# One class of candidates per row for strips 0 to 13, unsure rows settled in the tail, other gather lots

## Chip, core and metric

The kernel runs on one core of a Trainium2 chip. The metric is device time in microseconds (us), the median of several runs. Engines are named as in the profile: PE (matmul; PEld its weight loads), DVE (vector), ACT (scalar), POOL (GpSimd) and SP, whose queue loads the matrix.

## What is computed

The reference takes x (8192 x 64) and a sparse weighted adjacency matrix adj (8192 x 8192, float32, 268 MB) and applies two layers, each on a layer-normalised and rectified h:

```python
h = jnp.maximum(_layernorm(x, axis=-1), 0.0)
x = x + tanh([h, t] @ W1 + b1) @ W2 + b2 + adj @ (h @ B.T) - rowsum(adj) * (h @ B.T)
h = jnp.maximum(_layernorm(x, axis=-1), 0.0)
feats = h @ W                                   # 8 heads of 8
scores = leaky_relu(a_self[i] + a_neigh[j]) - 1e10 * (1 - adj[i, j])
x = x + relu(softmax_j(scores) @ feats + bias)
```

The mask is 1e10 times one minus the weight. Where the largest weight of a row leads the second by enough, the softmax is one at that neighbour and zero elsewhere, so the second layer is a gather: row i takes relu(feats + bias) of the column with its largest weight.

## The kernel before

**Strips.** The matrix, transposed and tiled on the host, comes in 16 strips (S) of 512 rows (W), each in 8 chunks of 2 MB, into a ring of four buffers. SP issues a load (L313 to L318) when PE (pe_chunk), ACT (half_done) and DVE (pair_done) are through with the buffer. A strip has four rows per partition (TB = 4).

**Per chunk.** PE multiplies it by h (`products`, L1032) and sums its rows (L1040, or L1050 on pairs that DVE added, L731). ACT casts it to float16 (`halve`, L544), and DVE folds the casts into a running maximum (`fold_chunk`, L738 and L742). DVE's order in a strip is written by hand (`strip`): pairs 0 and 1, the first fold, the candidates of the strip two back, the second fold, the classes of the strip before, and so on.

**Finding the largest weight.** Folding leaves, for each row, the maximum of each of 128 classes of 64 neighbouring columns. `search_classes` finds the top classes in float16 (L765, L769) and writes the row numbers of the first two (cls_row, L773). POOL fetches those two classes, 64 floats each, from adj in float32 (`fetch_rows`, L447): eight indirect DMAs of 128 rows of 256 B a strip. `search_candidates` finds the maximum of the 128 candidates (L786, L790) and the column, into best (L793 to L798).

**The gather.** relu(feats + bias) of each strip is stored to agg_dram (`store_agg`, L442). From strip 11 on POOL's order is written out: WINDOWS gives lots (known, t0, t1). In each, POOL adds b2 (L436), fetches half of the candidates of strip `known`, waits for the gathers of the previous lot, stores strip known - 1, fetches the rest, and gathers rows t0 to t1 per partition (L461) from the table, in which strips below `known` are stored. Rows whose best lies in a later strip read zeros and are late; up to SLOTS = 8 of them per partition are gathered after the last store (L490) and added to the output with a scatter (L499).

**The tail.** After the loop: `search_candidates(14)`, `search_classes(15)`, `residual(15)` (L806 to L819, waits for ACT's copy L602 of PE's results L1073 to L1080), `scale_h1` (L823, waits for ACT's deviation L615, L617), then the list of late rows (L887 to L908), agg_last (L912), its store by SP (L337), POOL's late gathers, scatters and last gathers, DVE's last addition (L918), and a test that the short cut held (L931 to L957). If it did not, a general path runs, which is slow.

## Time and profile before

| | us |
|---|---|
| median of 3 runs | 792.81 (790.75 to 794.08) |
| the profiled execution | 791.36 |
| its span, first to last instruction | 789.6 |
| busy: PE, DVE, ACT, POOL | 684.5, 652.1, 594.3, 388.5 |

Mean granted TensorE clock 0.948. A page has parts by number: 2 is the span in 40 slices, 3 the DMA queues, 5 groups of instructions with the idle time of the engine before them and what ended it. A timeline lists instructions in order of time; "x4" merges four.

### The profile page before, as it was taken

Reading aid. Unit: us, or ns where it says so; the run is one execution under the profiler, and the core shown is the slowest. Engines: PE = TensorE matmul, PEld = TensorE weight load, DVE = VectorE, ACT = ScalarE, POOL = GpSimd, SP = SyncE. Lnnn points to the kernel's source line nnn. Section 1 sums busy time; section 2 is a strip of 40 time slices with the busy share of each in tenths; the row PEclk is TensorE's granted clock in tenths of the full one; section 3 lists DMA queues with packets and bytes.
Section 4 is the critical chain, followed back from the end, with each engine's and each line's share of the span. In section 5 each row is a group of like instructions: output and inputs, shape, how many; then the busy total and the mean of one; then the engine's idle time right before and its main releaser. Section 6 shows DMA issues by size and latency. Waiting matters only on the chain.

```text
span 789.6 us, 13173 instructions
## 1 busy us (share of the span) xinstructions
PE 684.5 (87%) x4470; PEld 244.7 (31%) x4470; DVE 652.1 (83%) x944; ACT 594.3 (75%) x507; POOL 388.5 (49%) x281
## 2 busy tenths in 40 slices
PE   4899999999999999999999999999999999992100
PEld 1233333333333233333333333323233333332000
DVE  4586899999999989989899999999988989893420
ACT  3798888898879798888888887979797878880200
POOL 7000544434170807051443526070888888887574
PEclk9999999999999999999999999999999999995555
DMA  8999899999999999999999999999999999951161
GB/s 329 415 417 430 340 429 395 420 397 422 399 403 432 377 429 377 432 375 432 375 423 399 424 389 415 431 376 430 366 423 388 427 392 411 416 200 28 35 122 20
DMA packets 34544, 287.02 MB, mean 363 GB/s; under 512 B 7456, under 2 KB 13968, under 8 KB 18016
## 3 DMA queue, kind: packets, MB, share of 16 engines
q1 hardware_dynamic: 23168, 275.00, 84.4%
q0 software_dynamic: 9056, 9.73, 4.9%
q10 hardware_dynamic: 2304, 2.10, 0.8%
q8 instruction: 7, 0.11, 0.1%
q14 instruction: 9, 0.07, 0.0%
HBM read 279.46 MB, written 7.34 MB: 363 GB/s over the span
## 4 chain that ended last, share of the span: by engine, by line
PE 34%; DMA 27%; DVE 16%; issue 15%; ACT 3%; POOL 3%; DVEq 1%; SPq 0%; POOLq 0%; ACTq 0%
DMA ring<-in_adj_t 26%; PE acc L1032 22%; DVE work L742 6%; PE row_sums L1040 4%; PE row_sums L1050 4%; DVE work L731 4%; ACT work L544 2%; POOL out L499 2%; DVE work L738 1%; POOL work L490 1%; DVE work L748 1%; DVE idx_cls L769 1%; PE ps_xb L1080 1%; PE ps_acc L1073 1%; DMA work<-agg_dram,late_from 1%
## 5 line engine op out<-in xcount | busy, mean ns | idle before, releaser
L544 ACT CAST work<-ring 128x4096 f16<-128x4096 f32 x128 | 458.6, 3603 | 64.4 <-DMA ring<-in_adj_t 26.3
L1032 PE MATMUL acc<-ring,x_pb 128*64 128x512 f32 x2048 | 455.9, 596 | 14.8 <-DMA ring<-in_adj_t 14.8
L447 POOL DMA_INDIRECT cand<-in_adj,cls_row x128 | 226.7, 1771 | 86.9 <-DVE cls_row L773 49.0
L742 DVE TENSOR_TENSOR work<-work 128x4096 f16<-128x4096 f16 x96 | 221.6, 2309 | 22.5 <-ACT work L544 19.5
L1032 PEld LDWEIGHTS acc<-ring,x_pb 128*64 128x64 f32 x2048 | 140.4, 137 | 318.2 <-issue 280.1
L731 DVE TENSOR_TENSOR work<-ring 128x2048 f32<-128x2048 f32 x90 | 208.8, 2334 | 8.0 <-DMA ring<-in_adj_t 3.6
L442 POOL DMA_DIRECT2D agg_dram<-agg x15 | 9.0, 601 | 228.4 <-ACT agg L577 185.2
L461 POOL DMA_INDIRECT gathered<-agg_dram,best x64 | 85.5, 1336 | 20.9 <-issue 20.9
L1050 PE MATMUL row_sums<-work,ones_cols 128*32 128x512 f32 x720 | 89.5, 598 | 0.2 <-DVE work L731 0.2
L1040 PE MATMUL row_sums<-ring,ones_cols 128*32 128x512 f32 x608 | 72.9, 616 | 14.0 <-DMA ring<-in_adj_t 14.0
L436 POOL TENSOR_TENSOR x_tq<-x_tq,b_row 128x256 f32 (+1 forms) x16 | 30.4, 1902 | 42.5 <-DMA x_tq<-in_x 42.3
L738 DVE TENSOR_TENSOR work<-work 128x4096 f16<-128x4096 f16 x16 | 36.6, 2286 | 2.3 <-ACT work L544 2.3
L1040 PEld LDWEIGHTS row_sums<-ring,ones_cols 128*32 128x32 f32 x608 | 19.4, 112 | 57.2 <-issue 53.9
L1050 PEld LDWEIGHTS row_sums<-work,ones_cols 128*32 128x32 f32 x720 | 18.7, 109 | 54.3 <-issue 54.2
L615 ACT ACTIVATE tmp<-cen 128x64 f32<-128x64 f32 x64 | 15.6, 244 | 20.9 <-DVE cen L819 14.5
L602 ACT COPY acc_tq<-ps_acc 128x260 f32<-128x260 f32 x16 | 5.9, 369 | 24.8 <-remote 24.4
L1095 PE MATMUL ps_hid<-ident,h 128*128 128x128 f32 x2 | 0.7, 434 | 25.4 <-DVE rstd L823 25.4
L806 DVE TENSOR_TENSOR tmp<-ps_xb,acc_tq 128x256 f32<-128x256 f32 x16 | 6.7, 417 | 19.2 <-issue 19.2
L748 DVE TENSOR_TENSOR work<-work 128x2048 f16<-128x2048 f16 x16 | 19.6, 1225 | 2.3
L562 ACT ACT_TABLE_LOAD x16 | 20.5, 1283 | 0.3
L617 ACT ACT_TABLE_LOAD x16 | 20.5, 1283 | 0.3
L918 DVE TENSOR_TENSOR gathered<-gathered,x_tq 128x256 f32<-128x256 f32 (+1 forms) x3 | 4.7, 1573 | 18.5 <-DMA gathered<-agg_dram,best 18.5
(140 smaller groups left out, 503.7 us busy)
## 6 DMA issues: line engine op xcount, KB each, us to landing
ring<-in_adj_t SPq DMA_DIRECT2D x128, 2048.0 KB
agg_dram<-agg POOLq DMA_DIRECT2D x20, 128.0 KB, 20.1
x_tq<-in_x SPq DMA_DIRECT2D x1, 2048.0 KB, 16.3
cand<-in_adj,cls_row POOLq DMA_INDIRECT x128
raw_dram<-feat_stage ACTq DMA_DIRECT2D x16, 128.0 KB, 9.6
out<-gathered SPq DMA_DIRECT2D x1, 1792.0 KB
x_pb<-in_x SPq DMA_DIRECT2D x1, 1536.0 KB, 14.5
gathered<-agg_dram,best POOLq DMA_INDIRECT x64
```

Source lines behind the costliest of these rows:

```text
L436: pool.tensor_tensor(x1, x1, b2_row[:, :].unsqueeze(1).to_broadcast([P, TB, D]), ALU.add).then_inc(x_b2_done, 1)
L447: pool.indirect_dma_start(out=cand[:, k, g * NB:(g + 1) * NB], out_offset=None, in_=classes, in_offset=bass.IndirectOffsetOnAxis(ap=cls_ro ...
L461: pool.indirect_dma_start(out=gathered[:, t, :], out_offset=None, in_=agg_dram, in_offset=bass.IndirectOffsetOnAxis(ap=best[:, t:t + 1], a ...
L544: act.copy(half_chunk[c % 2], slot(c)).then_inc(half_done, 1)
L562: act.activation(hidden[:, :], ps_hid[:, :], ACT.Tanh, bias=hid_bias[:, 3:4])\
L731: dve.tensor_tensor(pairs[i % PBUF], slot(c)[:, 0:HALF], slot(c)[:, HALF:2 * HALF], ALU.add)\
L738: dve.tensor_tensor(half_max, half_chunk[0], half_chunk[1], ALU.max).then_inc(max_done, 1)
L742: dve.tensor_tensor(half_max, half_max, half_chunk[c % 2], ALU.max).then_inc(max_done, 1)
L748: dve.tensor_tensor(half_max[:, 0:4 * W], half_max[:, 0:4 * W], half_max[:, 4 * W:8 * W], ALU.max)\
L1032: last = pe.matmul(acc[0][at:at + D, :], x_pb[:, c * CB + b, :], slot(c)[:, b * W:(b + 1) * W], start=(c == 0 and b < 2), stop=(c == NC - ...
L1040: last = pe.matmul(row_sums[at:at + QUAD, :], ones_cols[:, :], slot(c)[:, b * W:(b + 1) * W], start=(c == 0 and b < 4), stop=(c == NC - 1 ...
L1050: last = pe.matmul(row_sums[b * QUAD:(b + 1) * QUAD, :], ones_cols[:, :], pairs[i % PBUF][:, b * W:(b + 1) * W], start=(c == 0), stop=(c = ...
```

## The change

For strips 0 to 13 POOL fetches only the first class of each row. DVE then finds the maximum of its 64 values and compares it with an upper bound of the second class (its float16 maximum, widened). Where the bound is not below, the row is unsure: best is set to 8192, a row of zeros that agg_dram now has, so the row counts as late. After the loop `unsure_rows` picks one unsure row per partition, POOL fetches both of its classes, and `resolve_unsure` finds its column, which is merged into the list of late rows. Strips 14 and 15 keep both classes (`search_both`). The number of unsure rows per partition and the lead of the resolved row enter the test at the end. The lots become 12, 16, 18, 10 and 4 gathers instead of 14, 14, 14, 14 and 4; in the last lot POOL's order is new, and `scale_h1(15)` moves behind the late marks and `resolve_unsure`. Left out below: declarations, semaphores, and lines that repeat a pattern; of the new tests (11 small operations on `good`) two stand.

```diff
-WINDOWS = ((11, 0, 14), (12, 14, 28), (13, 28, 42), (14, 42, 56), (15, 56, 60))
+WINDOWS = ((11, 0, 12), (12, 12, 28), (13, 28, 46), (14, 46, 56), (15, 56, 60))
 EARLY = 14 * TB
+SURE = 14
+KEPT = SURE * TB
...
-        agg_dram = nc.dram_tensor("agg_dram", (N, D), F32, kind="Internal").ap()
+        agg_dram = nc.dram_tensor("agg_dram", (N + P, D), F32, kind="Internal").ap()
...
+            pool.iota(span_t[:, :], pattern=[[-P * P, KEPT]], base=(NB - 1) * P * P, channel_multiplier=0).then_inc(pool_const, 1)
+            pool.wait_ge(pool_const, 17)
...
+            pool.dma_start(agg_dram[N:N + P, :], agg[:, 0:D]).then_inc(zero_stored, 16)
...
-            def fetch_rows(k0, k1):
+            def fetch_rows(k0, k1, cls=1):
                 for k in range(k0, k1):
-                    for g in range(CLS):
+                    for g in range(cls):
                         pool.indirect_dma_start(
                             out=cand[:, k, g * NB:(g + 1) * NB], out_offset=None, in_=classes,
                             in_offset=bass.IndirectOffsetOnAxis(ap=cls_row[:, k, g:g + 1], axis=0),
                         ).then_inc(cand_in, 16)
-            def fetch_candidates(s, k0=0, k1=TB):
+            def fetch_candidates(s, k0=0, k1=TB, cls=1):
                 pool.wait_ge(cls_row_done, s + 1)
                 pool.sem_inc(pool_past, 1)
-                fetch_rows(k0, k1)
+                fetch_rows(k0, k1, cls)
...
-            for w, (known, t0, t1) in enumerate(WINDOWS):
-                if known + 1 < S:
-                    add_b2(known + 1)
-                fetch_candidates(known, 0, TB // 2)
+            for w, (known, t0, t1) in enumerate(WINDOWS[:-1]):
+                cls = 1 if known < SURE else CLS
+                add_b2(known + 1)
+                fetch_candidates(known, 0, TB // 2, cls)
                 if w:
                     pool.wait_ge(got[w - 1], 16 * (WINDOWS[w - 1][2] - WINDOWS[w - 1][1]))
                 store_agg(known - 1)
-                if known < S - 1:
-                    fetch_rows(TB // 2, TB)
+                fetch_rows(TB // 2, TB, cls)
                 pool.wait_ge(agg_stored, 16 * known)
                 gather(w, t0, t1)
-            fetch_rows(TB // 2, TB)
+            pool.wait_ge(unsure_row_done, 1)
+            for g in range(CLS):
+                pool.indirect_dma_start(
+                    out=unsure_cand[:, g * NB:(g + 1) * NB], out_offset=None, in_=classes,
+                    in_offset=bass.IndirectOffsetOnAxis(ap=unsure_row[:, g:g + 1], axis=0),
+                ).then_inc(unsure_in, 16)
+            w = len(WINDOWS) - 1
+            pool.wait_ge(got[w - 1], 16 * (WINDOWS[w - 1][2] - WINDOWS[w - 1][1]))
+            store_agg(S - 2)
+            fetch_candidates(S - 1, 0, TB, CLS)
+            pool.wait_ge(agg_stored, 16 * (S - 1))
+            gather(w, WINDOWS[w][1], WINDOWS[w][2])
...
-                dve.scalar_tensor_tensor(cls_step[:, :], idx_cls[:, :, 1], -1.0, idx_cls[:, :, 0], ALU.add, ALU.subtract)\
-                    .then_inc(cls_step_done, 1)
+            def search(s, n):
+                for k in range(TB):
+                    dve.max(top_cand[:, k, :], cand[:, k, 0:n]).then_inc(cand_top, 1)
+                dve.wait_ge(cand_top, s * TB + TB)
+                dve.sem_inc(dve_past, 1)
+                for k in range(TB):
+                    dve.max_index(idx_cand[:, k, :], top_cand[:, k, :], cand[:, k, 0:n]).then_inc(cand_done, 1)
+                dve.wait_ge(cand_done, s * TB + TB)
             def search_candidates(s, first=False):
                 ts = bass.ds(s * TB, TB)
-                dve.wait_ge(cand_in, s * (16 * TB * CLS) + 16 * TB * CLS)
+                dve.wait_ge(cand_in, s * (16 * TB) + 16 * TB)
                 if not first:
                     dve.wait_ge(lead_kept, s)
                 dve.sem_inc(dve_past, 1)
...
+                search(s, NB)
+                dve.tensor_scalar(bound[:, :], top_cls[:, :, 1], 1.0 + ROUND, FLOOR, ALU.mult, ALU.add).then_inc(pick, 1)
                 dve.scalar_tensor_tensor(in_class[:, :], idx_cls[:, :, 0], float(NB), idx_cand[:, :, 0], ALU.mult, ALU.add)\
                     .then_inc(pick, 1)
-                dve.wait_ge(pick, s * 2 + 2)
+                dve.scalar_tensor_tensor(classes_of[:, ts], idx_cls[:, :, 0], float(P), idx_cls[:, :, 1], ALU.mult, ALU.add)\
+                    .then_inc(pick, 1)
+                dve.wait_ge(pick, s * 4 + 3)
+                dve.tensor_tensor(unsure[:, ts], bound[:, :], top_cand[:, :, 0], ALU.is_ge).then_inc(pick, 1)
+                dve.wait_ge(pick, s * 4 + 4)
+                dve.sem_inc(dve_past, 1)
+                dve.scalar_tensor_tensor(best[:, ts], unsure[:, ts], float(N), in_class[:, :], ALU.mult, ALU.max)\
+                    .then_inc(best_done, 1)
+            def search_both(s):
+                ts = slice(s * TB, s * TB + TB)
+                n = s - SURE
+                dve.wait_ge(cand_in, 16 * TB * (SURE + CLS * (n + 1)))
+                dve.wait_ge(lead_kept, s)
+                search(s, CLS * NB)
...
+            def unsure_rows():
+                dve.wait_ge(best_done, SURE)
+                dve.wait_ge(pool_const, 17)
+                dve.tensor_tensor(unsure_key[:, :], classes_of[:, :], span_t[:, :], ALU.add).then_inc(unsure_chain, 1)
+                dve.tensor_reduce(good[:, 6:7], unsure[:, :], AX.X, ALU.add).then_inc(unsure_chain, 1)
+                dve.wait_ge(unsure_chain, 2)
+                dve.tensor_tensor(unsure_key[:, :], unsure_key[:, :], unsure[:, :], ALU.mult).then_inc(unsure_chain, 1)
+                dve.wait_ge(unsure_chain, 3)
+                dve.max(unsure_top[:, :], unsure_key[:, :]).then_inc(unsure_chain, 1)
+                dve.wait_ge(unsure_chain, 4)
+                dve.tensor_copy(unsure_int[:, :], unsure_top[:, 0:1]).then_inc(unsure_chain, 1)
+                dve.wait_ge(unsure_chain, 5)
+                dve.tensor_scalar(unsure_s[:, :], unsure_int[:, :], 14, NB - TB, ALU.logical_shift_right, ALU.bitwise_and)\
+                    .then_inc(unsure_chain, 1)
...
+                dve.wait_ge(unsure_chain, 9)
+                dve.scalar_tensor_tensor(unsure_at[:, :], unsure_s[:, :], -float(P), late_base[:, 0:1], ALU.mult, ALU.add)\
+                    .then_inc(unsure_chain, 1)
+                dve.wait_ge(unsure_chain, 10)
+                dve.tensor_tensor(unsure_node[:, :], unsure_at[:, :], unsure_k[:, :], ALU.subtract).then_inc(unsure_chain, 1)
+                dve.wait_ge(unsure_chain, 11)
+                dve.scalar_tensor_tensor(unsure_row[:, :], unsure_node[:, :].to_broadcast([P, CLS]), float(P), unsure_cls[:, :],
+                                         ALU.mult, ALU.add).then_inc(unsure_row_done, 1)
+            def resolve_unsure():
+                dve.wait_ge(unsure_in, 16 * CLS)
+                dve.max(unsure_lead[:, :], unsure_cand[:, :]).then_inc(unsure_chain, 1)
+                dve.scalar_tensor_tensor(unsure_step[:, :], unsure_cls[:, 1:2], -1.0, unsure_cls[:, 0:1], ALU.add, ALU.subtract)\
+                    .then_inc(unsure_chain, 1)
+                dve.wait_ge(unsure_chain, 13)
+                dve.max_index(unsure_idx[:, :], unsure_lead[:, :], unsure_cand[:, :]).then_inc(unsure_chain, 1)
...
+                dve.wait_ge(unsure_chain, 17)
+                dve.tensor_scalar(unsure_move[:, :], unsure_move[:, :], -float(N), None, ALU.add).then_inc(unsure_done, 1)
...
-            search_candidates(S - 2)
+            unsure_rows()
+            search_both(S - 2)
             search_classes(S - 1)
             residual(S - 1)
-            scale_h1(S - 1)
             dve.wait_ge(best_done, S - 1)
-            dve.wait_ge(pool_const, 16)
             for known, t0, t1 in WINDOWS:
                 dve.tensor_scalar(is_late[:, t0:t1], best[:, t0:t1], float(known * W), None, ALU.is_ge)\
                     .then_inc(late_chain, 1)
             dve.tensor_tensor(late_key[:, :], best[:, 0:LATE], late_span[:, :], ALU.add).then_inc(late_chain, 1)
-            n = len(WINDOWS) + 1
+            resolve_unsure()
+            scale_h1(S - 1)
+            n = len(WINDOWS) + 2
+            dve.wait_ge(unsure_done, 1)
+            dve.wait_ge(late_chain, n - 1)
+            dve.scalar_tensor_tensor(late_key[:, 0:KEPT], unsure[:, :], unsure_move[:, :], late_key[:, 0:KEPT], ALU.mult, ALU.add)\
+                .then_inc(late_chain, 1)
...
-            search_candidates(S - 1)
+            search_both(S - 1)
...
+            dve.tensor_reduce(good[:, 7:8], lead[:, :, 0], AX.X, ALU.min).then_inc(third_chain, 1)
+            dve.tensor_scalar(good[:, 8:10], unsure_lead[:, 0:2], -1.0, MASK, ALU.add, ALU.mult).then_inc(third_chain, 1)
...
-            dve.tensor_scalar(good[:, 2:3], good[:, 0:1], LEAD, None, ALU.is_ge).then_inc(end_chain, 1)
+            dve.wait_ge(third_chain, 11)
+            dve.scalar_tensor_tensor(good[:, 2:3], good[:, 0:1], LEAD, good[:, 14:15], ALU.is_ge, ALU.mult).then_inc(end_chain, 1)
```

## Rows read from the trace of the kernel before

**Rows 1.** Page, part 2: the span in 40 slices, busy tenths and granted clock.

```profile
PE   4899999999999999999999999999999999992100
PEclk9999999999999999999999999999999999995555
DMA  8999899999999999999999999999999999951161
```

**Rows 2.** Busy us by stretch (one strip each, instructions in brackets), clock, DMA share, GB/s.

```profile
165.20:207.60 42.40, 41.51 (x279) 14.89 (x276) 39.56 (x54) 36.00 (x31) 15.46 (x10) 1.00 0.99 411
...
293.80:335.10 41.30, 41.30 (x279) 14.97 (x276) 38.91 (x51) 34.45 (x30) 16.04 (x10) 1.00 0.98 405
...
506.10:549.40 43.30, 41.60 (x278) 14.75 (x274) 39.99 (x55) 36.64 (x32) 17.62 (x10) 1.00 0.99 407
549.40:593.10 43.70, 41.70 (x279) 14.79 (x276) 39.87 (x55) 36.02 (x31) 33.12 (x20) 1.00 0.97 397
...
635.60:679.20 43.60, 42.23 (x279) 15.23 (x276) 39.20 (x55) 36.80 (x31) 37.03 (x25) 1.00 1.00 404
...
712.10:789.60 77.50, 7.31 (x64) 5.39 (x64) 20.35 (x85) 4.70 (x18) 47.97 (x44) 0.50 0.29 52
```

**Rows 3.** Page, part 3: DMA queues: packets, MB, share of 16 engines' span.

```profile
q1 hardware_dynamic: 23168, 275.00, 84.4%
q0 software_dynamic: 9056, 9.73, 4.9%
```

**Rows 4.** Page, part 5: groups on POOL: busy, mean ns, idle before them.

```profile
L447 POOL DMA_INDIRECT cand<-in_adj,cls_row x128 | 226.7, 1771 | 86.9 <-DVE cls_row L773 49.0
L436 POOL TENSOR_TENSOR x_tq<-x_tq,b_row 128x256 f32 (+1 forms) x16 | 30.4, 1902 | 42.5 <-DMA x_tq<-in_x 42.3
```

**Rows 5.** Timeline, DVE, 330 to 337 us: start, length, instruction, idle before it.

```profile
330.45 2.28 DVE L738 TENSOR_TENSOR work<-work 128x4096 f16<-128x4096 f16 x1
...
332.99 0.87 DVE L786 MAX8 top_cand<-cand 128x8 f32<-128x128 f32 x4
...
336.70 2.29 DVE L742 TENSOR_TENSOR work<-work 128x4096 f16<-128x4096 f16 x1 [0.99 <-ACT work L544]
```

**Rows 6.** Timeline, ACT, same stretch.

```profile
332.85 7.12 ACT L544 CAST work<-ring 128x4096 f16<-128x4096 f32 x2 [0.94 <-DVE work L738]
```

**Rows 7.** Groups of instructions, shapes apart, DVE: busy, mean ns, idle.

```profile
L786 DVE MAX8 top_cand<-cand 128x8 f32<-128x128 f32 x64 | 13.8, 277 | 0.0
...
L795 DVE SCALAR_TENSOR_TENSOR in_class<-idx_cls,idx_cand 128x4 f32<-128x4 uint32 x16 | 2.5, 157 | 0.0
...
L895 DVE MAX8 late_top<-late_key 128x8 f32<-128x60 f32 x1 | 0.2, 215 | 0.0
```

**Rows 8.** Timeline, all engines, 717 to 790 us.

```profile
717.04 0.37 PE L1080 MATMUL ps_xb<-b_t_diag,h_strip 128*128 128x128 f32 x1
...
736.23 0.38 ACT L602 COPY acc_tq<-ps_acc 128x260 f32<-128x260 f32 x1 [23.34 <-remote]
...
736.64 0.42 DVE L806 TENSOR_TENSOR tmp<-ps_xb,acc_tq 128x256 f32<-128x256 f32 x1 [19.19 <-issue]
...
741.63 0.95 POOL L447 DMA_INDIRECT cand<-in_adj,cls_row  x1 [0.30 <-issue]
...
741.99 0.18 DVE L823 RECIPROCAL rstd<-stat 128x4 f32<-128x4 f32 x1 [2.74 <-ACT stat L617]
...
745.38 0.42 DVE L912 TENSOR_TENSOR agg_last<-ps_feat,bias_row 128x256 f32<-128x256 f32 x1 [0.78 <-PE ps_feat L1102]
...
748.32 2.43 POOL L490 DMA_INDIRECT work<-agg_dram,late_from  x1 [5.75 <-DMA agg_dram<-agg_last]
...
774.97 0.42 DVE L918 TENSOR_TENSOR gathered<-gathered,x_tq 128x256 f32<-128x256 f32 x1 [18.54 <-DMA gathered<-agg_dram,best]
```

**Rows 9.** Timeline, POOL, around the fetches of strips 13 and 14.

```profile
646.44 3.06 POOL L447 DMA_INDIRECT cand<-in_adj,cls_row  x1
...
690.08 0.96 POOL L447 DMA_INDIRECT cand<-in_adj,cls_row  x1 [0.16 <-issue]
```

More of the change, by code:

```diff
@@ L135, in build @@
         cls_step = sb("cls_step", [P, TB])
+        bound = sb("bound", [P, TB])
+        unsure = sb("unsure", [P, KEPT])
+        classes_of = sb("classes_of", [P, KEPT])
+        unsure_key = sb("unsure_key", [P, KEPT])
+        unsure_top = sb("unsure_top", [P, 8])
+        unsure_int = sb("unsure_int", [P, 1], U32)
+        unsure_s = sb("unsure_s", [P, 1], U32)
+        unsure_k = sb("unsure_k", [P, 1], U32)
+        unsure_cls = sb("unsure_cls", [P, CLS], U32)
+        unsure_at = sb("unsure_at", [P, 1])
+        unsure_node = sb("unsure_node", [P, 1])
+        unsure_row = sb("unsure_row", [P, CLS], U32)
+        unsure_cand = sb("unsure_cand", [P, CLS * NB])
+        unsure_lead = sb("unsure_lead", [P, 8])
+        unsure_idx = sb("unsure_idx", [P, 8], U32)
+        unsure_step = sb("unsure_step", [P, 1])
+        unsure_second = sb("unsure_second", [P, 1])
+        unsure_first = sb("unsure_first", [P, 1])
+        unsure_move = sb("unsure_move", [P, 1])
+        span_t = sb("span_t", [P, KEPT], I32)
         at_second = sb("at_second", [P, TB])
@@ L141, in build @@
         gap = sb("gap", [P, 4, NB])
-        good = sb("good", [P, 6])
+        good = sb("good", [P, 16])
         agg = sb("agg", [P, TB * D])
@@ L197, in build @@
         raw_stored = sem("raw_stored")
-        cls_step_done = sem("cls_step_done")
         pick = sem("pick")
+        pick_two = sem("pick_two")
+        unsure_chain = sem("unsure_chain")
+        unsure_row_done = sem("unsure_row_done")
+        unsure_in = sem("unsure_in")
+        unsure_done = sem("unsure_done")
         gen_raw_in = sem("gen_raw_in")
@@ L274, in build @@
         out_by_q = out.rearrange("(s q k) d -> q s (k d)", q=P, k=TB)
-        agg_by_q = agg_dram.rearrange("(s q k) d -> q s (k d)", q=P, k=TB)
+        agg_by_q = agg_dram[0:N, :].rearrange("(s q k) d -> q s (k d)", q=P, k=TB)
         classes = adj.rearrange("i (p b) -> (i p) b", b=NB)
@@ L571, in rectify @@
                 if first:
-                    act.wait_ge(zero_stored, 16 * (S - WINDOWS[0][0]))
+                    act.wait_ge(zero_stored, 16 * (S - WINDOWS[0][0] + 1))
                 else:
@@ L784, in search_candidates @@
                 dve.sem_inc(dve_past, 1)
-                for k in range(TB):
-                    dve.max(top_cand[:, k, :], cand[:, k, :]).then_inc(cand_top, 1)
-                dve.wait_ge(cand_top, s * TB + TB)
-                dve.sem_inc(dve_past, 1)
-                for k in range(TB):
-                    dve.max_index(idx_cand[:, k, :], top_cand[:, k, :], cand[:, k, :]).then_inc(cand_done, 1)
-                dve.wait_ge(cand_done, s * TB + TB)
-                dve.scalar_tensor_tensor(at_second[:, :], idx_cand[:, :, 0], float(NB), cls_step[:, :], ALU.is_ge, ALU.mult)\
-                    .then_inc(pick, 1)
+                search(s, NB)
@@ new lines, in search_candidates @@
+                dve.wait_ge(pick, s * 4 + 3)
[10 more added lines that the diff above has]
+                search(s, CLS * NB)
+                dve.scalar_tensor_tensor(cls_step[:, :], idx_cls[:, :, 1], -1.0, idx_cls[:, :, 0], ALU.add, ALU.subtract)\
+                    .then_inc(pick_two, 1)
+                dve.scalar_tensor_tensor(in_class[:, :], idx_cls[:, :, 0], float(NB), idx_cand[:, :, 0], ALU.mult, ALU.add)\
+                    .then_inc(pick_two, 1)
+                dve.wait_ge(pick_two, n * 3 + 1)
+                dve.scalar_tensor_tensor(at_second[:, :], idx_cand[:, :, 0], float(NB), cls_step[:, :], ALU.is_ge, ALU.mult)\
+                    .then_inc(pick_two, 1)
+                dve.wait_ge(pick_two, n * 3 + 3)
```

26 lines of the change are left out of this document (24 added, 2 removed).

## The prediction

> **What bounds the kernel now.** I read the slices first: PE and the DMA engines stand at nine tenths from the second slice to the 35th, at the full granted clock, then comes a tail in which little runs [rows 1], 77.5 us from the last turn of the maxima at 712.1 [rows 2]. So there are two stages to cost. For the first I asked for the strips one by one [rows 2]. The nine strips from 165.2 to 549.4 take 384.2 us, 42.69 each; the DMA engines are 97 to 99% busy in them, PE 41.3 to 41.6 us, DVE 39 to 40 us. No single engine is the bound: in the fastest strip PE is busy for all of its 41.30 us, and in the others it waits about 1.2 us, mostly for a chunk. The three strips from 549.4 to 679.2, in which POOL issues 22 row transfers a strip where it issued 8 before, take 129.8 us, 43.27 each, with the DMA engines at 0.97 to 1.00. The fetches are thus paid, if at all, as DMA time between chunks.
>
> In the tail the order of events counts [rows 8]. PE's last matmul of ps_xb starts at 717.04; the copy that needs it starts on ACT at 736.23 and DVE goes on at 736.64 after 19.19 us without work. From there a chain runs through the normalising (L823 at 741.99), features, agg_last (745.38), its store, and POOL's eight gathers of late rows from 748.32, behind which POOL scatters until the end. POOL's other work ended with the fetch at 741.63, and it sat idle 5.75 us.
>
> **The change, part by part.** *Fetches.* Fourteen strips lose four fetches each, 56 of 128. On POOL one takes 1.77 us on average [rows 4] plus 0.30 to issue [rows 8], some 8 us of POOL a strip; POOL waits for DVE anyway in the looped strips, so that is worth nothing there. On the DMA engines: a fetch is 128 rows of 256 B, 32 KB, so 56 are 1.84 MB of the 9.73 MB of queue q0, whose packets took 4.9% of 789.6 us, 38.7 us [rows 3]. By bytes that is 38.7 x 1.84/9.73 = 7.3 us. From below, the strips say less: 14 more row transfers made a strip 43.27 - 42.69 = 0.58 us longer, 0.041 us each, and 56 x 0.041 = 2.3 us [rows 2]. The first price holds if the DMA engines are always the last to be ready, the second is what the whole strip passes on while PE and DVE are nearly as full. Neither excludes zero or a loss in a single strip, but over 14 I see no reason for a loss. I take the middle, 4.7 us, since the DMA share is 0.97 to 0.99 and PE's idle time ends with a chunk; ends 2.3 and 7.3.
>
> Per MB, queue q0 takes 4.9/9.73 = 0.50% of the span and q1 84.4/275 = 0.31%, so small rows cost 1.6 times their bytes [rows 3]. The Trainium skill (DMA: Bandwidth & Descriptors, Specifications) states that a transfer under 512 B is read, modified and written and so misses line rate; by that rule a 256 B row would count about double, which by this page would put the removal above the share by bytes if the rest of q0 had long rows. The rows show the direction of it, not the factor.
>
> *Search on DVE.* The maxima and indices run over 64 values instead of 128: a maximum over 60 took 0.215 us against 0.277 [rows 7], so four of each save about 0.5 us. Two small operations go (cls_step, at_second), three come (bound, classes_of, unsure), each near 0.16 us like L795 [rows 7], and one more wait inside the chain, which I take as a tenth or two. Net -0.5 to +0.1 us a strip. It counts for nothing: the search stands between the fold at 330.45 and the fold at 336.70, and the latter waits 0.99 us for ACT's cast [rows 5, 6]. Only an addition above 0.99 us would show.
>
> *Lots.* The gathers move from 14, 14, 14, 14, 4 to 12, 16, 18, 10, 4. Before, POOL's round from 646.44 to 690.08 is 43.6 us for 8 fetches and 14 gathers [rows 9], 1.9 us each after the addition of b2 (1.90, [rows 4]). The rounds after have 4 + 12, 4 + 16, 4 + 18 and 8 + 10 transfers: 32, 40, 44 and 36 us against strips of 43, so POOL is on time for strip 14. The row transfers per strip in this stretch fall from 22 to 16, 20 and 22; they are in the 56.
>
> *After the loop, POOL.* Two fetches for the unsure rows come first, then a wait for the fourth lot, the store of strip 14, eight fetches for strip 15, four gathers. In all POOL has 12 fetches fewer in the written-out part and two more, so it is done some 5 us ahead of 742.6; even if the new waits (unsure_row_done, then got) cost it 4 us, it is not later than before, and 5.75 us of idle time stand behind [rows 8]. One iota and one 32 KB store at the start hide behind 42.3 us in which POOL waits for x_tq [rows 4].
>
> *After the loop, DVE.* unsure_rows is a chain of 12 small operations, about 12 x 0.2 = 2.5 us, put ahead of search_both for strip 14; it delays the classes of strip 15, and with them POOL's last fetches, by that. On DVE it lies in the 19.19 us before L806 [rows 8]; without that cover it costs 2.5. resolve_unsure (a maximum and an index search over 128 values, each near L786's 0.28 us [rows 7], and five small ones: 0.56 + 5 x 0.2 = 1.6 us) and the moved late marks (six operations issued without a wait between them, 0.6 us) stand before scale_h1, in the 2.74 us in which DVE waits for ACT's deviation [rows 8]: 2.2 us, it just fits; cost 0 to 0.3. The merge into late_key adds 0.22 us where DVE has 0.78 us to spare before agg_last [rows 8]. Eleven checks at the end, 2 us, lie in the 18.54 us wait for the last gathers [rows 8].
>
> **Sum.** The profiled execution took 791.36 us around a span of 789.6. 791.36 - 4.7 + 0 (tail, 0 to 0.3) = 786.7. The median of the runs shown, 792.81, is 1.45 above it: 788.1 on that scale, with ends 785.5 and 790.5.
>
> **Rivals.** *Nothing measurable.* PE and DVE are as full as the DMA engines (41.30 of 41.30 us in the fastest strip), so what DMA saves turns into waits for free chunk buffers. For: a maximum of several nearly equal loads gives less per transfer the fewer there are, and 0.041 us is the price at the loaded end. Against: PE's 1.2 us a strip. It gives 0 to 2.3 us, 790.5 to 792.8, with noise to 794.
>
> *The stop of 19 us shrinks.* The rows name no cause for it: PE's matmul is there, its release arrives late ("remote"), while POOL's transfers run [rows 8]. If it hangs on POOL's stream, which ends earlier now, the tail moves up until POOL itself is the bound, near 737 instead of 748.3: up to 11 us more, 777 us. Against: POOL still issues at the same rate there.
>
> *Slower: DVE is stopped in the same way.* The stop stands in the straight code that PE runs behind its loop. DVE's straight code behind its loop grows by about half; if a stop as long as PE's falls between L806 and L912, nothing hides it: 788.1 + 19.2 = 807. It decides if DVE's idle time there exceeds the 2.74 us before L823 and has no engine behind it. Against: DVE shows no such stop behind its loop now. The Trainium skill (Runtime: NRT & Kernel Launch, Instruction fetch mechanics) says that code is fetched in 16 KiB blocks ahead of a straight run and that a branch out of the fetched window stalls the engine; by that rule PE's stop is a fetch and DVE's longer code could meet one too; the trace does not contradict it.
>
> *The change doesn't do what it says.* An unsure row too many in one partition would send the kernel through the general path, which no row here prices. By the inputs 13 of the 7168 rows of strips 0 to 13 are unsure, never two in a partition, and no partition has over 8 late rows. Nearly excluded.
>
> **Numbers.** Half a per cent, 4.0 us, is about what a measurement of this kernel can tell from no change; the bounds are 788.85 and 796.8. Forecast 0.54, of which 0.38 falls below 788.85 and 0.16 above; nothing measurable 0.25; stop shrinks 0.07; DVE stopped 0.13; general path 0.01. Faster 0.38 + 0.07 = 0.45, same 0.16 + 0.25 = 0.41, slower 0.14. The range takes in the forecast's ends, the rival without effect up to 794.5, and part of the shrinking stop down to 781.5; left out are 0.14 slower and about 0.04 faster.
>
> **What would show it.** Right: 72 rows of L447's successor and two unsure fetches; strips before the 12th at 42.2 to 42.5 us with the DMA share lower by about 0.01 and PE's idle time near 0.8 us; the later ones near 42.8; DVE's wait before its third fold at 1 us or more; POOL idle sooner; the tail of 77.5 us [rows 2] the same within 1 us. Strips unchanged at 42.7 with a lower DMA share mean the first rival. A gain in the tail, with DVE's 19.19 us shorter, means the second; a new idle time of DVE behind 737 us the third. A loss in the looped strips would make the argument wrong altogether.

## The result, and the profile after

The changed kernel took 794.11 us (median of 17 runs, 789.47 to 797.84) against 790.75 us for the kernel before in the same comparison (17 runs, 786.96 to 794.08): ratio 1.0052, 95% interval 1.0035 to 1.0069. It is slower by half a per cent; a time of 788.1 us, faster than the kernel before, was forecast. The profiled execution took 792.68 us around a span of 791.1 us (before: 791.36 around 789.6).

The page of the changed kernel, its slices and its queues [rows 1, 3]:

```profile
PE   4998999999999999999999999999999999980100
PEclk9999999999999999999999999999999999995555
DMA  8999999999999999999999999999999999931062
...
q1 hardware_dynamic: 23168, 275.00, 84.2%
q0 software_dynamic: 7360, 7.99, 4.3%
```

Queue q0 lost 1696 packets and 1.74 MB. The stretches, cut at the same events (turn of the maxima to turn of the maxima) as [rows 2]:

```profile
162.69:205.21 42.52, 41.65 (x278) 14.79 (x275) 39.15 (x55) 35.94 (x31) 8.57 (x6) 1.00 0.98 405
290.40:332.80 42.40, 41.75 (x278) 14.70 (x275) 39.17 (x55) 35.87 (x31) 8.56 (x6) 1.00 0.97 401
503.62:546.10 42.48, 41.65 (x278) 14.78 (x274) 39.07 (x55) 35.95 (x31) 8.55 (x6) 1.00 0.98 404
546.10:589.46 43.36, 41.66 (x278) 14.78 (x275) 39.62 (x57) 37.14 (x31) 27.83 (x18) 1.00 0.97 397
632.01:675.17 43.16, 41.90 (x278) 15.12 (x275) 39.13 (x55) 36.21 (x31) 35.49 (x22) 1.00 1.01 407
707.78:791.10 83.32, 6.76 (x64) 5.03 (x64) 24.39 (x115) 4.70 (x18) 46.25 (x42) 0.51 0.27 47
```

The nine strips to 546.10 take 383.4 us, 42.60 each (before 42.69); the last turn of the maxima comes at 707.78 in place of 712.10, 4.3 us sooner. But the tail is 83.3 us long where it was 77.5. The groups on POOL [rows 4] and two groups that wait:

```profile
L475 POOL DMA_INDIRECT cand<-in_adj,cls_row x72 | 122.0, 1694 | 87.3 <-DVE cls_row L812 65.8
...
L641 ACT COPY acc_tq<-ps_acc 128x260 f32<-128x260 f32 x16 | 5.9, 370 | 33.3 <-remote 32.0
...
L918 DVE TENSOR_TENSOR tmp<-ps_xb,acc_tq 128x256 f32<-128x256 f32 x16 | 6.7, 419 | 22.9 <-ACT acc_tq L641 22.9
```

The timeline of the tail [rows 8] (start, length, engine, line, idle before it):

```profile
713.39 0.37 PE L1211 MATMUL ps_xb<-b_t_diag,h_strip 128*128 128x128 f32 x1 [0.83 <-issue]
...
733.48 0.95 POOL L489 DMA_INDIRECT gathered<-agg_dram,best  x1 [0.30 <-issue]
...
737.57 0.38 ACT L641 COPY acc_tq<-ps_acc 128x260 f32<-128x260 f32 x1 [28.98 <-remote]
737.97 0.43 DVE L918 TENSOR_TENSOR tmp<-ps_xb,acc_tq 128x256 f32<-128x256 f32 x1 [22.89 <-ACT acc_tq L641]
743.29 0.18 DVE L935 RECIPROCAL rstd<-stat 128x4 f32<-128x4 f32 x1 [0.92 <-ACT stat L656]
746.67 0.42 DVE L1029 TENSOR_TENSOR agg_last<-ps_feat,bias_row 128x256 f32<-128x256 f32 x1 [1.09 <-PE ps_feat L1233]
749.57 2.48 POOL L529 DMA_INDIRECT work<-agg_dram,late_from  x1 [15.14 <-DMA agg_dram<-agg_last]
776.69 0.43 DVE L1035 TENSOR_TENSOR gathered<-gathered,x_tq 128x256 f32<-128x256 f32 x1 [17.87 <-DMA gathered<-agg_dram,best]
```

Behind the copy acc_tq nothing has changed: from it to the end it is 53.5 us here (791.1 - 737.57) and 53.4 before (789.6 - 736.23). Ahead of it, TensorE's stop (last turn of the maxima to that copy) has grown from 24.13 us (736.23 - 712.10) to 29.79 (737.57 - 707.78), 5.66 us. That is more than the 4.3 us gained; with 0.1 us behind the copy that makes the 1.5 us by which the span grew. The matmul that releases the copy is recorded as ended at 713.76 us (717.41 before), and both traces record its semaphore update only 0.02 us ahead of the copy, 23.8 us later (18.8 before). So it is TensorE's release that comes late, and ScalarE and VectorE wait for it. The question for the runs was why the stop grew.

### The profile page after: what moved, and what is told of

Same layout as the page of the kernel before. It is cut to its first block, busy times and chain, and to the rows that moved or that the text cites. A ratio compares the mean times of both kernels' runs of the same rounds, so it can differ in the third digit from the quotient of the medians.

```text
span 791.1 us, 13206 instructions
## 1 busy us (share of the span) xinstructions
PE 683.4 (86%) x4470; PEld 244.0 (31%) x4470; DVE 652.5 (82%) x987; ACT 593.8 (75%) x507; POOL 278.8 (35%) x229
## 4 chain that ended last, share of the span: by engine, by line
DVE 28%; issue 23%; DMA 11%; ACT 5%; PE 5%; another core or an unknown queue 4%; POOL 3%; DVEq 2%; POOLq 0%; SPq 0%; ACTq 0%
DVE work L781 11%; DMA ring<-in_adj_t 10%; DVE work L770 6%; ACT work L583 4%; PE acc L1163 3%; DVE work L777 3%; DVE work L787 2%; POOL out L538 2%; DVE idx_cls L808 1%; DVE work L790 1%; DVE top_cls L804 1%; POOL work L529 1%; PE row_sums L1181 1%; DVE x_tq L924 1%
## 5 line engine op out<-in xcount | busy, mean ns | idle before, releaser
L781 DVE TENSOR_TENSOR work<-work 128x4096 f16<-128x4096 f16 x96 | 220.0, 2291 | 22.8 <-ACT work L583 20.8
L770 DVE TENSOR_TENSOR work<-ring 128x2048 f32<-128x2048 f32 x90 | 204.7, 2288 | 7.8 <-issue 3.6
L475 POOL DMA_INDIRECT cand<-in_adj,cls_row x72 | 122.0, 1694 | 87.3 <-DVE cls_row L812 65.8
L489 POOL DMA_INDIRECT gathered<-agg_dram,best x64 | 95.0, 1485 | 25.1 <-issue 18.6
L1181 PEld LDWEIGHTS row_sums<-work,ones_cols 128*32 128x32 f32 x720 | 18.8, 109 | 53.9 <-issue 53.5
L464 POOL TENSOR_TENSOR x_tq<-x_tq,b_row 128x256 f32 (+1 forms) x16 | 13.3, 832 | 41.4 <-DMA x_tq<-in_x 41.2
```

What stands on the lines that cost most here:

```text
L475: pool.indirect_dma_start(out=cand[:, k, g * NB:(g + 1) * NB], out_offset=None, in_=classes, in_offset=bass.IndirectOffsetOnAxis(ap=cls_ro ...
L489: pool.indirect_dma_start(out=gathered[:, t, :], out_offset=None, in_=agg_dram, in_offset=bass.IndirectOffsetOnAxis(ap=best[:, t:t + 1], a ...
L770: dve.tensor_tensor(pairs[i % PBUF], slot(c)[:, 0:HALF], slot(c)[:, HALF:2 * HALF], ALU.add)\
L781: dve.tensor_tensor(half_max, half_max, half_chunk[c % 2], ALU.max).then_inc(max_done, 1)
L1181: last = pe.matmul(row_sums[b * QUAD:(b + 1) * QUAD, :], ones_cols[:, :], pairs[i % PBUF][:, b * W:(b + 1) * W], start=(c == 0), stop=(c = ...
```

## Experiments

Eighteen more kernels ran, on six chips: e1 to e3 on one, c1, c2, e4 and e5 on the next, then e6, e7 and c3, the four c4, then e8, e9 and c5, and e10 alone. Ratios are to the kernel before, run between them on the same chip.

**POOL held.** If TensorE stops because POOL issues transfers back to back, a pause of POOL should end it. Both kernels got a wait in POOL's last lot, the changed one behind the unsure fetches, the other ahead of strip 15's:

```diff
+            pool.wait_ge(acc_turned, S)
             w = len(WINDOWS) - 1
...
+                if known == S - 1:
+                    pool.wait_ge(acc_turned, S)
                 fetch_candidates(known, 0, TB // 2)
```

> The changed kernel, with one wait added on POOL: behind the two fetches for the unsure rows it waits until PE's last products of strip 15 are released (acc_turned). Theory A (PE's stop behind its loop lasts as long as POOL issues row transfers back to back): POOL pauses near 719 us, the stop ends by about 723 instead of 737.5, then POOL's remaining 13 transfers, 16 us, end near 738 and the late gathers start there instead of at 749.6: about 782 us, 11 to 14 us under the changed kernel. Theory B (the stop has a cause of its own that POOL does not touch): it ends near 737.5 again, POOL's transfers run from there to 754 instead of ending at 734.4, and the kernel takes 4 to 6 us longer, 798 to 800 us.

> The kernel before, with the same wait on POOL ahead of the fetches for strip 15, near 725.8 us. Theory A: the stop ends by about 729 instead of 736.2, POOL has 13 transfers left, 17 us, and is done near 746, so the late gathers start near 746 to 747 instead of 748.3: 1 to 2 us faster at most, and the copy of PE's results on ACT starts near 729. Theory B: the stop ends at 736.2, POOL is done near 753, about 5 us slower.

**TensorE's code shifted.** On the same chip, 256 waits that are already fulfilled, in place of one, make TensorE's program 127 instructions longer ahead of its loop and so move the loop and the code behind it:

```diff
-            pe.wait_ge(pool_const, 3)
+            for _ in range(256):
+                pe.wait_ge(pool_const, 3)
```

> The changed kernel with 127 more instructions on PE ahead of its loop (waits that are already fulfilled), so that PE's loop and the code behind it lie 127 instructions further on. Theory C (the stop is a load of PE's code that lies at a fixed place of its program): the stop behind the loop moves to another instruction or vanishes; if it vanishes, the copy of PE's results on ACT starts near 714 instead of 737.6, POOL becomes the bound at 734.4 and the kernel takes 779 to 783 us. Theory D (it hangs on what PE does, not on where its code lies): the stop stays before ACT's copy, near 737, and the time within 2 us of the changed kernel.

Measured: 784.83 us (ratio 0.9972, 0.9958 to 0.9985), 786.86 us (1.0002, 0.9980 to 1.0023) and 784.72 us (0.9971, 0.9955 to 0.9987). From last turn to copy it was 2.63, 3.98 and 4.17 us: no stop in any of the three. But in the first it had gone before POOL reached its wait (POOL was still issuing at 715.5, the copy stood at 710.71). An edit that works before it acts is no cause, so the unchanged kernels had to be run.

**Controls.** Both kernels unchanged, the shifted code in the kernel before, and the changed kernel with the old lots (14, 14, 14, 14, 4):

> The kernel before, unchanged, as a control for the length of TensorE's stop behind its loop (last turn of the maxima to ScalarE's copy acc_tq), which was 24.13 us in the first trace. Theory A (the stop is what TensorE's way out of its loop costs while POOL's transfers are issued back to back) and theory C (it hangs on where TensorE's code lies against its loop) both expect 19 to 25 us again, since neither the code nor the order is changed. Theory V (it varies from chip to chip or run to run) allows any value from 3 to 30 us; a short stop here, under 8 us, would take the force from the two runs with POOL held.

> The changed kernel, unchanged, as a control on this chip. Theories A and C: a stop near 29.8 us as in the first trace, and a time 0.3 to 0.7% above the kernel before. Theory V: the stop can be anything, and with it the ratio moves: with no stop in either kernel the change should be 3 to 5 us faster (ratio 0.994 to 0.997).

> The kernel before with the same 256 fulfilled waits ahead of TensorE's loop that took the stop out of the changed kernel. Theory C (code position): the stop is gone here too, 4 us from the last turn to the copy in place of 24, and the time falls below the kernel before by what the stop had cost at the end, 1 to 4 us; the changed kernel with the same padding (784.7 us against 787.5 for before) is then the fair partner, and the change's own worth is the difference of the two. Theory A (POOL's transfers): nothing in POOL's stream is changed, so the stop stays at 19 to 25 us and the time within 1 us of the kernel before.

> The changed kernel with the lots of gathers of the kernel before (14, 14, 14, 14 and 4 blocks). Only POOL's order in the tail is changed: 10 gathers less between the fetches of strips 13 and 14, 4 more in the lot behind. Theory A (the stop ends when POOL's back-to-back stream first pauses): the stop changes with the stream, by several us either way. Theory C: the stop stays as in the changed kernel, to 1 us, and the time within 1.5 us of it.

The kernel before, unchanged (c1_before), then the changed one on a later chip (c5_after):

```profile
714.19 0.71 PE L1080 MATMUL ps_xb<-b_t_diag,h_strip 128*128 128x128 f32 x4
...
714.94 0.38 ACT L602 COPY acc_tq<-ps_acc 128x260 f32<-128x260 f32 x1 [1.83 <-PE ps_xb L1080]
```

```profile
713.77 1.17 PE L1211 MATMUL ps_xb<-b_t_diag,h_strip 128*128 128x128 f32 x4
...
714.98 0.38 ACT L641 COPY acc_tq<-ps_acc 128x260 f32<-128x260 f32 x1 [3.36 <-PE ps_xb L1211]
```

The copy follows the last matmul at once, released by it and not by "remote". Last turn to copy: 2.62 us in the kernel before (787.72 us, a single run), 3.73 in the changed one, 4.10 with shifted code, 2.62 with the old lots. And the changed kernel, unedited, is faster: 784.25 us, ratio 0.9978 (0.9963 to 0.9993), 2.3 us where 3 to 5 were expected. The shifted code gives 786.07 us (0.9987, 0.9970 to 1.0003), as without it. Theories A and C fall as causes that hold everywhere. One thing the shifted code did move: the kernels with unshifted code all have a read of 16 KB on an instruction queue within 2 us of the last turn, the three with shifted code have none there; the stop is absent either way. The old lots cost: 789.88 us (1.0039, 1.0020 to 1.0057), tail 77.2 us against 72.3.

**A stop of known length.** ScalarE makes 20 copies that nobody needs ahead of acc_tq, in both kernels:

```diff
             rectify(S - 2, False)
+            for i in range(20):
+                act.wait_ge(act_held, i)
+                act.copy(held[:, :], ident[:, 0:1].to_broadcast([P, 1024])).then_inc(act_held, 1)
             keep_turned(S - 1)
```

> The kernel before with a stop of a known length put in by hand: in the tail ScalarE makes 20 copies of 128x1024 (by the 128x4096 cast's 3.6 us about 1 us each, 20 us in all) ahead of its copy acc_tq, so that everything behind it comes as late as it did behind TensorE's stop of 24.13 us, on chips where that stop isn't seen. Theory T (the end is the later of two chains: POOL's stream of transfers, and the chain behind acc_tq, which needs 53.4 us from the copy to the end): with the copy near 736 us the span is 789 to 790 us and the time 2 to 4 us over the kernel before. Theory U (the first measurement's times come from something else than the stop): the time stays within 1 us of the kernel before.

> The same 20 copies in the changed kernel, so both kernels have a stop of equal length. Theory T: the copy ends with the loop's end plus the same time as in the kernel before with the copies, the end is again 53 to 54 us behind it, and so the changed kernel is faster than that one by what its loop gives, 1 to 4 us; that the change came out slower in the first measurement was then wholly the 5.65 us by which the stop itself was longer. A rival (the tail with its unsure rows and other lots stands a late copy worse than the tail before): the copy to the end takes over 56 us here, and the changed kernel is no faster.

> The changed kernel, unchanged, once more, on whichever chip this is. If TensorE's stop belongs to a chip (theory V), a chip without it gives a stop under 5 us and a ratio of 0.996 to 0.999; a chip with it gives 28 to 31 us and a ratio near 1.005. If the stop belongs to the order or the code of the changed kernel (theories A and C) it is 28 to 31 us on every chip; one unchanged run without it has already spoken against that.

The kernel before with the copies, then the changed one (ScalarE's timeline):

```profile
735.34 0.37 ACT L604 COPY acc_tq<-ps_acc 128x260 f32<-128x260 f32 x1
```

```profile
729.80 0.37 ACT L643 COPY acc_tq<-ps_acc 128x260 f32<-128x260 f32 x1
```

Their last turns were at 713.27 and 707.74, so from last turn to copy it is 22.07 and 22.06 us. TensorE's own release came 0.01 us behind its last matmul in both. The spans are 789.1 and 783.0: 53.8 and 53.2 us behind the copy, as in the first traces (53.4 and 53.5). Theory T holds for the traces. The medians are 788.48 us (ratio 1.0015, 0.9993 to 1.0037) and 786.96 us (0.9997, 0.9975 to 1.0020). The first is 1.8 us above the kernel before, just under the 2 to 4 us expected and alone not clear of theory U; the second is 2.9 us above c3_after. The tails had grown by 2.2 and 2.8 us. So with stops of one length the changed kernel is not the slower one. Their difference, 1.5 us, lies inside the two intervals, and the two profiled executions exaggerate it: e7's is the fastest of its ten, e6's one of its slower ones. c3_after without a stop (2.62 us): 784.08 us, ratio 0.9958 (0.9939 to 0.9977).

**Once more for the stop.** Four kernels on a fourth chip:

> The kernel before, unchanged, looking again for TensorE's stop (24.13 us in the first trace; none on the three chips since, 2.6 to 4.2 us from the last turn of the maxima to the copy acc_tq). Theory V (it belongs to the chip or its session): under 5 us here if this chip is like those three, or 20 to 25 us with a span near 789.6 us.

> The changed kernel, unchanged. Theory V: both kernels have the stop here or neither. Without it a ratio of 0.995 to 0.999, tail 72 to 73 us from the last turn; with it a ratio of 1.003 to 1.007 and a tail near 83 us.

> The changed kernel with POOL held behind the unsure fetches until ps_acc is turned. On a chip with the stop: theory A (POOL's back-to-back transfers keep TensorE's code away) expects the stop to end within 3 us of POOL's holding, so near 718 to 722 us; theory C expects 28 to 31 us. On a chip without it: nothing, 782 to 786 us.

> The changed kernel with the 256 fulfilled waits ahead of TensorE's loop. On a chip with the stop: theory C expects it gone or of another length by over 5 us; theory A expects 26 to 30 us as without them. On a chip without it: nothing, 783 to 787 us.

No stop in any: 4.04, 3.57, 3.42 and 2.63 us. The kernel before took 789.51 us in its profiled run (its 13 timed ones: median 786.10); the changed kernel, unedited, 783.93 us, ratio 0.9970 (0.9955 to 0.9986). The other two, a single run each: 783.66 and 783.72 us. What the stop hangs on could not be tried, since it did not come.

**What the parts are worth without the stop.** The fetches alone put back, and the lots alone moved:

```diff
                         ).then_inc(cand_in, 16)
+                    if cls == 1:
+                        pool.indirect_dma_start(
+                            out=spare[:, k, :], out_offset=None, in_=classes,
+                            in_offset=bass.IndirectOffsetOnAxis(ap=cls_row[:, k, 1:2], axis=0),
+                        ).then_inc(cand_in, 16)
```

> The changed kernel with the 56 removed fetches put back (the second class's 256 B of every row of strips 0 to 13, into a buffer that nobody reads, waited for as before); the search over 64 values, the unsure tail and the new lots stay. Theory F (the fetches are what the loop gained, and POOL's time in strips 12 to 14 gained from them too): loop from first to last turn 1.5 to 2.5 us longer than the changed kernel's 629.1 us, and, since four more fetches of 1 to 2 us stand ahead of each of the lots 12 and 13, POOL comes to strip 14's fetches 4 to 8 us later and the tail grows by as much, to 76 to 80 us: 789 to 793 us in all. Rival: what the prediction had, the fetches are worth their DMA time alone (2.3 to 7.3 us), all in the loop, and the tail stays at 72 to 73 us.

> The kernel before with the changed kernel's lots (12, 16, 18, 10 and 4 blocks) and all else as it was. Theory F: with 8 fetches a strip POOL is full from strip 12 on, so the gathers moved from the lot of strip 14 into the lot of strip 13 only move its lateness: the tail stays at 72 to 75 us and the time within 1.5 us of the kernel before. Rival (the lots alone are worth what they were worth in the changed kernel, where the old lots cost 4.9 us of tail): tail near 69 us and 4 to 5 us faster than before.

> The changed kernel, unchanged, as partner of the two on the same chip: ratio 0.996 to 0.999 and a tail of 72 to 73 us if TensorE's stop is absent here too, 1.003 to 1.007 and 83 us if this is a chip with it.

With the fetches back: 795.08 us, ratio 1.0092 (1.0063 to 1.0121); its partner without them 785.65 us, 0.9981 (0.9965 to 0.9997). So the 56 fetches are worth 9.4 us by the medians; theory F has it right, though the median lies above its 789 to 793 us. Of the 7.9 us between the two spans, the loop (first to last turn) takes 2.8 (632.37 us against 629.60, one trace each, 0.049 us a fetch), the tail 4.2 (77.0 against 72.8). The tail's part is POOL: when the classes of strip 14 are known and when POOL fetches their rows, first in the changed kernel, then with the fetches put back, then in the kernel before with the new lots.

```profile
683.72 1.95 POOL L489 DMA_INDIRECT gathered<-agg_dram,best  x1 [0.30 <-issue]
685.69 1.95 POOL L464 TENSOR_TENSOR x_tq<-x_tq,b_row 128x256 f32<-128x256 f32 x1
687.79 0.97 POOL L475 DMA_INDIRECT cand<-in_adj,cls_row  x1 [0.15 <-issue]
```

```profile
697.33 0.97 POOL L476 DMA_INDIRECT cand<-in_adj,cls_row  x1 [0.16 <-issue]
```

```profile
691.80 0.75 POOL L436 TENSOR_TENSOR x_tq<-x_tq,b_row 128x256 f32<-128x256 f32 x1
692.70 0.97 POOL L447 DMA_INDIRECT cand<-in_adj,cls_row  x1 [0.16 <-issue]
```

The classes (DVE's cls_row) stood at 682.32, 685.29 and 680.78, so POOL is 5.5, 12.0 and 11.9 us late. From its first fetch for strip 14 on, POOL issues nearly without a pause to the end, and in the unedited kernels without a stop the end is 95 to 97 us behind that fetch. The new lots in the kernel before: profiled 783.99 us, but median 788.2 us over a spread of 783.0 to 791.5, ratio 1.0011 (0.9983 to 1.0039). POOL needs only 89.7 us from its first fetch for strip 14 to the end there, with four gathers fewer, but starts 2.3 us later than the kernel before did (692.70 against 690.35 in c1_before); the tail is 72.6 us where the rival wanted 69, and the median rules out 4 us of gain. That profiled execution is one of the fastest three of ten.

e8_after_spare and e9_before_newlots have the same lots and, for the strips, the same number of fetches. They differ in the unsure rows' tail with its two fetches, POOL's new order in the last lot and the shorter search. From the first fetch for strip 14 to the end the first needs 94.2 us, the second 89.7, and the medians are 6.9 us apart (each uncertain by about 2). So this part of the change costs 4 us or more where POOL's stream sets the end, and the fetches saved pay for it.

**POOL's order in the tail.** The timeline of c5_after shows POOL standing still between the last lot and the late gathers; in the kernel before (c1_before, second) four fetches lie there:

```profile
739.93 0.95 POOL L489 DMA_INDIRECT gathered<-agg_dram,best  x1 [0.30 <-issue]
744.43 0.95 POOL L529 DMA_INDIRECT work<-agg_dram,late_from  x1 [3.54 <-DMA agg_dram<-agg_last]
```

```profile
740.50 0.95 POOL L461 DMA_INDIRECT gathered<-agg_dram,best  x1 [0.30 <-issue]
741.75 0.95 POOL L447 DMA_INDIRECT cand<-in_adj,cls_row  x1 [0.30 <-issue]
743.01 0.95 POOL L447 DMA_INDIRECT cand<-in_adj,cls_row  x1 [0.30 <-issue]
744.26 0.95 POOL L447 DMA_INDIRECT cand<-in_adj,cls_row  x1 [0.30 <-issue]
745.51 0.95 POOL L447 DMA_INDIRECT cand<-in_adj,cls_row  x1 [0.30 <-issue]
```

```diff
-            fetch_candidates(S - 1, 0, TB, CLS)
+            fetch_candidates(S - 1, 0, TB // 2, CLS)
             pool.wait_ge(agg_stored, 16 * (S - 1))
             gather(w, WINDOWS[w][1], WINDOWS[w][2])
+            fetch_rows(TB // 2, TB, CLS)
```

> The changed kernel with the fetches for the second half of strip 15 issued behind the gathers of the last lot again, as the kernel before has them. Theory O (in the changed kernel's order POOL stands still for 3.54 us between the last lot's gathers and the late ones, because SyncE stores agg_last only once those gathers have landed; four fetches of 1.25 us between them would cover that): the still time goes, POOL's stream ends 3 to 3.5 us earlier, tail 69 to 70 us from the last turn against 72 to 73, and the time 3 to 3.5 us below the changed kernel, near 781 us, ratio 0.991 to 0.994. Rival (POOL's stream isn't what ends last, or the later fetches make DVE's last search late): within 1 us of the changed kernel, ratio 0.996 to 0.999. On a chip with TensorE's stop: no better than the changed kernel there.

```profile
736.15 0.95 POOL L489 DMA_INDIRECT gathered<-agg_dram,best  x1 [0.30 <-issue]
737.40 0.95 POOL L475 DMA_INDIRECT cand<-in_adj,cls_row  x1 [0.30 <-issue]
...
741.17 0.95 POOL L475 DMA_INDIRECT cand<-in_adj,cls_row  x1 [0.30 <-issue]
742.43 0.95 POOL L530 DMA_INDIRECT work<-agg_dram,late_from  x1 [0.30 <-issue]
```

The idle time is gone, the tail is 69.3 us, and the time 781.17 us, ratio 0.9931 (0.9912 to 0.9950): theory O. This is the best version of the study: its ratio lies below the four of the changed kernel (0.9958 to 0.9981), which was not run beside it. It had no stop (2.63 us); what it does behind one was not seen.

## Why the prediction was wrong

**The step that failed** is "tail, 0 to 0.3": that the tail would stay at 77.5 us within 1 us, with the stop of 19.19 us on DVE carried over as a constant of the program. The prediction named the stop, found no cause for it, let it shrink in one rival, and never let it grow. It grew by 5.66 us, more than the whole expected gain. The measured 794.11 us lies inside the stated range of 781.5 to 794.5 by luck: that end of the range was there for a change without effect, and the time came about by a longer stop. The delayed kernels show that the end hangs on the copy by 53 to 54 us in either kernel, and that stops of one length leave the changed kernel no slower. Adding up with the first stop's length, the changed kernel's span would have been 707.78 + 24.13 + 53.5 = 785.4 us.

What made the stop 30 us instead of 24 is open. It stood in both first traces and in none of the 18 taken since, on six chips, twelve of them of edited and six of unedited kernels. The times say that a stop of about that length stood in the other runs of the first comparison too. All 17 of the changed kernel (789.47 us and up) are slower than each of its 40 on the later chips (787.69 at most), and its median is 9.6 us above the mean of those four medians; the traces, tails of 83.3 us with the stop against 72.5 without, would make it 10.8. For the kernel before the medians are 4.1 us apart (790.75 against a mean of 786.62 on the same four chips), the tails 3.9 (77.5 against 73.6). That the stop belongs to that chip or session is the likeliest reading and only argued. With it absent, the change came out faster in four comparisons of four, at ratios of 0.9958 to 0.9981, with 2.3, 2.6, 2.2 and 1.5 us between the medians, 2.1 in the mean.

**The loop's term** of 4.7 us was too large. The last turn came 4.3 us sooner in the first trace, but first to last turn was 628.56 us against 631.23, 2.7 us less, and over five unchanged traces of the changed kernel (628.56, 630.01, 630.53, 629.05, 629.60) against three of the one before (631.23, 631.17, 631.80) it is 1.85 us. Put back, the fetches cost 2.8 us of loop. The strips' own price, 0.041 us a fetch, was the right end (0.049 by the fetches put back, 1.85 / 56 = 0.033 by the unchanged traces); the middle with the price by bytes was not. The forecast's own sign says the same: 42.2 to 42.5 us for the earlier strips and near 42.8 for the later three were to show it right, and they took 42.60 and 43.0 (129.07 / 3). The rival "nothing measurable", 0 to 2.3 us, was the nearer for the loop.

**POOL on time for strip 14** failed too, and the first traces hid it. The prediction's own sum gave 44 us for strip 13's lot against a strip of 43, and that was already late. In the first trace the lot took 47.2 us (638.31 to 685.55) against 43.2 from strip 13's classes to strip 14's: 22 transfers at about 2.0 us with the pause between them (the 1.9 of the prediction was nearly right), the addition of b2, and 1.4 us in which POOL waited for strip 12's store to land, which the sum left out. POOL came to strip 14's fetches 5.5 us behind its classes (3.7 in c3_after; 6.5 in the kernel before, 5.5 in c4_before, 685.36 to 690.87). Behind the stop that is free. Without the stop POOL's stream sets the end, and there the change does four things: four gathers fewer behind strip 14's fetches (5.0 us), no wait of 1.69 us for the store of strip 14, two fetches for the unsure rows more (2.5 us), and the idle time of 3.54 us that the new order of the last lot uncovers. So the tail term of 0 to 0.3 us would have been too small without the stop too. The prediction's "not later than before, and 5.75 us of idle time stand behind" held for POOL's work in the first trace (done at 734.4 against 742.6) and overlooked that SyncE stores agg_last only when the last lot has landed, with fewer transfers left to cover that.

**What held.** DVE's search stayed covered (its third fold waits 1.07 us for ACT at 334.21, 0.99 before [rows 5]). 72 fetches and two for unsure rows; unsure_rows took 2 us and lay inside the stop; resolve_unsure and the late marks fitted, with 0.92 us left before L935 of the 2.74 [rows 8]; agg_last waits 1.09 us. The DVE rival did not come: no idle time behind 737 us that another engine does not explain. Of the rule cited there (the Trainium skill, Runtime: NRT & Kernel Launch, Instruction fetch mechanics), the trace shows one 16 KB read on the instruction queue that the shifted code marks as TensorE's, 1.2 us behind the last turn, 1.47 us long; in c2_after the same read takes 1.36 us and there is no stop. A block fetch of that length is no account of 24 or 30 us.

## What to carry to other kernels

A wait whose releaser the profile can't name is no constant: before a tail is summed behind it, run the unchanged kernel again, on another chip if there is one, and forecast both the case with the wait and the case without. Where two chains end close together, cost the change in both; here the one that the first trace hid (POOL's stream) was the one that a reorder of four fetches could shorten by 3 us. And read off who waits for the last item of a lot (here SyncE's store) before moving other work out from behind it.

## What the runs showed of the hardware that was not expected

- The stop itself: TensorE's last recorded pass ends at 713.76 us and its release comes at 737.55, while 16 KB of its code had been read by 710.4 and POOL's transfers went on at 1.25 us each until 734.4; in the 18 later traces the release follows 0.01 to 0.02 us behind the pass. Cause open.
- POOL's issue of an indirect transfer stands still while VectorE runs its long addition of two SBUF operands. In c5_after (VectorE, then POOL):

```profile
728.66 3.87 DVE L1035 TENSOR_TENSOR gathered<-gathered,x_tq 128x3584 f32<-128x3584 f32 x1
```

```profile
727.68 0.95 POOL L475 DMA_INDIRECT cand<-in_adj,cls_row  x1 [0.30 <-issue]
728.93 4.42 POOL L475 DMA_INDIRECT cand<-in_adj,cls_row  x1 [0.30 <-issue]
```

  The transfer that takes 0.95 us elsewhere in this tail took 4.42, to 0.8 us behind the addition's end, so the addition costs POOL's stream 3.5 us. The Trainium skill (GPSIMD Engine Reference, Specifications) says that POOL's SBUF interfaces are shared with VectorE and contend with its instructions of two SBUF inputs; the trace agrees. Moving that addition off POOL's stream was not tried.
- Ahead of the tail too the price of a transfer goes with VectorE's long instructions of two SBUF operands (the additions of pairs, L770, and the maxima of the folds, L781) and not with the ring's loads. From c5_after: two of them; a POOL transfer beside them, and one with none beside it; and the stretch around the latter, with a DMA share of 1.03 at 422 GB/s:

```profile
659.78 2.29 DVE L770 TENSOR_TENSOR work<-ring 128x2048 f32<-128x2048 f32 x1
661.99 2.29 DVE L781 TENSOR_TENSOR work<-work 128x4096 f16<-128x4096 f16 x1
```

```profile
661.00 1.90 POOL L489 DMA_INDIRECT gathered<-agg_dram,best  x1 [0.31 <-issue]
...
676.21 0.95 POOL L489 DMA_INDIRECT gathered<-agg_dram,best  x1 [0.30 <-issue]
```

```profile
674.95:678.40 3.45, 3.45 (x30) 0.95 (x28) 2.08 (x13) 3.06 (x2) 2.84 (x3) 1.00 1.03 422
```

  Of the 115 transfers ahead of 712 us, the 90 beside such an instruction of over 1 us took 1.91 us in the mean, the other 25 took 1.01 (1.07 at most), with 0.3 us between two. The two go together in time in the trace; no run moved VectorE's work to show the cause.
